# Second layer's cross attention: the scores of two heads issued as a pair, each contracting 32 partitions

## What is computed

```python
def _mha(query, key, value, Wq, bq, Wk, bk, Wv, bv, Wa, ba, mask=None):
    q = (query @ Wq + bq).reshape(Nq, Tq, 16, 16)
    k, v = ...                                   # from the context: 375 rows
    attn = jnp.einsum('bthd,bshd->bhts', q, k) / np.sqrt(16)
    score = jax.nn.softmax(attn, axis=-1)
    y = jnp.einsum('bhts,bshd->bthd', score, v).reshape(Nq, Tq, 256)
    return y @ Wa + ba

t2 = _mha(tgt, tgt, tgt, ..., tgt_mask)          # own attention
x = _layer_norm(tgt + t2, ln1_g, ln1_b)
t2 = _mha(x, memory, memory, ...)                # cross attention
x = _layer_norm(x + t2, ln2_g, ln2_b)
t2 = relu(x @ lin1_W + lin1_b) @ lin2_W + lin2_b
return _layer_norm(x + t2, ln3_g, ln3_b)
```

## Time and profile before

| | us |
|---|---|
| median of 3 runs | 3871.56 |
| the three runs | 3872.68, 3871.56, 3820.96 |
| the profiled execution | 3822.77 |
| its span, first to last instruction | 3821.0 |
| TensorE busy in the span | 3584.9 (94%) |
| VectorE busy | 2020.9 (53%) |
| ScalarE busy | 1746.1 (46%) |
| GpSimd busy | 402.0 (11%) |
| mean granted TensorE clock | 0.963 of full |

### The profile page before, as it was taken

The page is one execution under the profiler, slowest core; times in us unless marked ns, Lnnn a source line. Parts: engine busy times, 40 slices in busy tenths (PEclk is TensorE's granted clock), DMA queues, the critical chain, the costliest instruction groups (busy, mean ns, idle before and its releaser), DMA issues. The chain is left out here.

```text
span 3821.0 us, 67697 instructions
## 1 busy us (share of the span) xinstructions
PE 3584.9 (94%) x21748; PEld 2729.5 (71%) x21748; DVE 2020.9 (53%) x6215; ACT 1746.1 (46%) x4893; POOL 402.0 (11%) x488
## 2 busy tenths in 40 slices
PE   8999999999989999999997999999999997888888
PEld 6778778887867888888775666666676674565565
DVE  4644555464445555556554445445445445657656
ACT  3544545454443333334333545555555453344444
POOL 2101101110101111101101000000000001211111
PEclk9999999999999999999998999999999998898999
DMA  5000000000040000000001000000000000000000
GB/s 199 4 11 14 9 9 12 14 4 12 6 134 12 13 13 13 7 6 13 13 3 49 8 15 8 8 14 8 8 14 8 8 10 14 11 26 13 13 26 5
DMA packets 58462, 75.11 MB, mean 20 GB/s; under 512 B 6752, under 2 KB 55584, under 8 KB 57024
## 3 DMA queue, kind: packets, MB, share of 16 engines
q1 hardware_dynamic: 58176, 71.45, 5.9%
HBM read 64.04 MB, written 7.40 MB: 19 GB/s over the span
## 5 line engine op out<-in xcount | busy, mean ns | idle before, releaser
L161 PE MATMUL l_bank<-l_xT,weights_of_layers_and 128*128 128x224 f32 x2816 | 619.5, 374 | 17.2 <-ACT l_xT L1161 8.0
L161 PEld LDWEIGHTS l_bank<-l_xT,weights_of_layers_and 128*128 128x128 f32 x2816 | 550.1, 201 | 54.0 <-ACT l_xT L1161 8.7
L614 ACT ACTIVATE l_pT<-l_bank 125x336 f32<-125x336 f32 (+2 forms) x736 | 347.1, 472 | 341.0 <-PE l_bank L546 330.3
L546 PEld LDWEIGHTS l_bank<-identity,l_p 112*125 112x125 f32 (+2 forms) x2336 | 334.8, 178 | 184.6 <-issue 96.8
L546 PE MATMUL l_bank<-identity,l_p 112*125 112x112 f32 (+2 forms) x2336 | 390.0, 279 | 21.6 <-DVE l_p L590 18.2
L631 ACT ACTIVATE l_p<-l_p,l_nm 112x375 f32<-112x375 f32 x384 | 233.4, 608 | 284.9 <-DVE l_nm L665 283.8
L161 PE MATMUL l_bank<-l_cT,weights_of_layers_and 128*128 128x375 f32 x832 | 306.3, 495 | 4.7 <-DVE l_z L1811 3.7
L161 PE MATMUL l_bank<-weights_of_layers_and,l_cT 128*125 128x256 f32 (+2 forms) x960 | 301.0, 451 | 0.2
L728 POOL TENSOR_TENSOR l_ve<-l_mv,eps 112x2 f32<-112x2 f32 (+1 forms) x89 | 17.3, 195 | 2548.7 <-DVE l_mv L722 2548.7
L590 DVE TENSOR_SCALAR l_p<-l_p,l_rs 112x375 f32<-112x375 f32 (+1 forms) x608 | 255.1, 420 | 21.7
L568 PEld LDWEIGHTS l_bank<-l_pT,l_cv 125*64 125x64 f32 (+1 forms) x3648 | 163.6, 131 | 138.7 <-issue 98.7
(11 more groups left out here) (253 smaller groups left out, 6118.6 us busy)
## 6 DMA issues: line engine op xcount, KB each, us to landing
l_cT<-in_ctx_turned SPq DMA_DIRECT2D x32, 375.0 KB, 3.4
l_cx<-in_ctx SPq DMA_DIRECT2D x16, 375.0 KB
context_rows<-in_ctx_reversed SPq DMA_DIRECT2D x16, 375.0 KB
tokens<-x_after_layer SPq DMA_DIRECT2D x25, 224.0 KB, 2.6
x_after_layer<-l_z SPq DMA_DIRECT2D x24, 224.0 KB, 2.4
weights_of_layers_and<-bias_lines_kept SPq DMA_DIRECT2D x1, 2625.0 KB, 16.3
weights_of_layers_and<-in_L_xattn_w_fused SPq DMA_DIRECT2D x1, 2048.0 KB, 10.7
weights_of_layers_and<-in_L_xattn_w_ff SPq DMA_DIRECT2D x1, 2048.0 KB, 12.7
```

The source lines that it names most:

```text
L161: last = pe.matmul(out, left, right, start=(k == 0), stop=(k == len(pairs) - 1))
L546: last = pe.transpose(TR.bank(m)[:ph.keys, g * ph.rows:(g + 1) * ph.rows], p[:ph.rows, m % self.p_slots, g * ph.keys:(g + 1) * ph.keys], i ...
L614: return act.activation(out, src, ACT.Copy)
```

## The change

For a phase that isn't grouped (L1's cross phase alone), `scores` does nothing in odd steps. In an even step k it waits for all that items k and k + 1 need, the banks of both among it, and then issues both scores one behind the other, into two banks, each with its own increment. `at` swaps the second and third head of each four, so the order of heads is 0, 2, 1, 3, 4, 6, 5, 7 and so on. `quarter` cuts both operands to the 32 partitions that hold the head and its neighbour, so that the two scores of a pair lie in different groups of 32 partitions (heads 0 and 1 in partitions 0 to 31, heads 2 and 3 in 32 to 63). Transposes, values and what the other engines do keep their order. In `Columns` the same was written with `abreast`, which is 1 everywhere, so that the other layers issue what they did.

```diff
     def at(self, k):
-        return self.batches[k // self.per_batch], k % self.per_batch
+        r = k % self.per_batch
+        if not self.grouped:
+            r += (0, 1, -1, 0)[r % G]
+        return self.batches[k // self.per_batch], r
...
         def scores(ph, k):
+            if not ph.grouped:
+                if k % 2 == 0:
+                    for n in (k, k + 1):
+                        for sem, count in S.free(i, ph.first + n, *ph.ready(n)):
+                            pe.wait_ge(sem, count)
+                    for n in (k, k + 1):
+                        pe.matmul(S.bank(ph.first + n)[:T, 0:S2], ph.q(*ph.at(n)), ph.k(*ph.at(n)), start=True, stop=True).then_inc(S.full.sem, 1)
+                return
             m = ph.first + k
...
-            if ph.grouped:
-                for g in range(G):
-                    last = pe.matmul(bank[:T, g * T:(g + 1) * T], ph.q(j, r * G + g), ph.k(j, r * G + g), start=True, stop=True)
-            else:
-                last = pe.matmul(bank[:T, 0:S2], ph.q(j, r), ph.k(j, r), start=True, stop=True)
+            for g in range(G):
+                last = pe.matmul(bank[:T, g * T:(g + 1) * T], ph.q(j, r * G + g), ph.k(j, r * G + g), start=True, stop=True)
...
+        def quarter(h, a):
+            n = h * DH % 128 // 32 * 32
+            return a[n:n + 32, :]
+
+        cross = Phase("c", False, H, DH, lambda j, h: quarter(h, qz[:, h // HEADS_PER_TILE, h % HEADS_PER_TILE, j * T:(j + 1) * T]),
+                      lambda j, h: quarter(h, ckT[:, j, h // HEADS_PER_TILE, :]), lambda j, h, t: cv[:, j, t, h, :], cross_ready, val_ready=cross_values_ready)
```

More of the change, by code:

```diff
@@ L430, in __init__ @@
     def __init__(self, name, items, dh, rows, q, k, val, ready, val_ready, place, out, bias=None, grouped=False, sides=2, tiles=CT,
-                 turned_by="act", emptied_by="dve", scaled_by="dve", ring=None):
+                 turned_by="act", emptied_by="dve", scaled_by="dve", ring=None, abreast=1):
+        self.abreast = abreast
         self.name, self.items, self.dh, self.rows, self.q, self.k, self.val, self.ready = name, items, dh, rows, q, k, val, ready
@@ L532, in scores @@
         def scores(ph, k):
[L533 to L539, removed]
+            if k % ph.abreast:
+                return
+            width, own = ph.keys * ph.tiles, range(k, k + ph.abreast)
+            for n in own:
+                for sem, count in S.free(i, ph.first + n, *ph.ready(n)):
+                    pe.wait_ge(sem, count)
+            for n in own:
+                for g in range(ph.n):
+                    last = pe.matmul(S.bank(ph.first + n)[:ph.rows, g * width:(g + 1) * width], ph.q(n, g), ph.k(n, g), start=True, stop=True)
+                last.then_inc(S.full.sem, 1)
         def turns(ph, k):
@@ L1469, in layer1 @@
                     bias=lambda r: wide(masked[:, :], 1, G), val_ready=own_values_ready)
-        cross = Phase("c", False, H, DH, lambda j, h: qz[:, h // HEADS_PER_TILE, h % HEADS_PER_TILE, j * T:(j + 1) * T],
-                      lambda j, h: ckT[:, j, h // HEADS_PER_TILE, :], lambda j, h, t: cv[:, j, t, h, :], cross_ready, val_ready=cross_values_ready)
+        def quarter(h, a):
[3 more added lines that the diff above has]
+                      lambda j, h: quarter(h, ckT[:, j, h // HEADS_PER_TILE, :]), lambda j, h, t: cv[:, j, t, h, :], cross_ready, val_ready=cross_values_ready)
         OWN = cross.items
```

## The result

| | before | after |
|---|---|---|
| median, us | 3846.73 (4 runs, 3820.96 to 3872.68) | 4121.59 (4 runs, 4116.16 to 4134.33) |
| span of the profiled execution | 3821.0 | 4123.7 |
| mean granted clock | 0.963 | 0.874 |

The change makes the kernel slower: ratio 1.0741, 95% interval 1.0672 to 1.0809 (the quotient of the two medians, 1.0715, lies inside it).

A forecast was written before the change was run, and what follows sets the result against it. TensorE, busy 94% of the span, was taken to set the pace. With the clock lost, cross adds 293 us and own 86, total 379 on the profiled 3822.77, giving 4202 us; range 4030 to 4300.

The forecast's parts named there:

- Overlap: L1 cross scores: a pair's two scores overlap fully, taking 0.63 us, a saving of 0.63 per pair.
- Switch and settled pair: L1 cross: switching between 32-partition groups and whole array costs 0.30 a pair; settled pair 2.75 us instead of 3.08.
- the held clock: Rival: clock stays 1.00 in cross despite the starting hole; 3797 us, or 3759 with free switches; chance 0.16.
- The wait: Start of each cross phase: pair (2, 3) waits for exponential 0, leaving TensorE a hole of 2.4 us.
- The clock falls about 4 us in: Each cross phase: granted clock drops to 0.50 about 4 us after its start.
- Because of the hole: Start of cross: about 1.2 us busy in the first 3.4, less than in either stall that cost the clock.
- It won't come back by itself: Cross, mostly loads, and own: clock remains at 0.50 until the projections after own.
- Its rival: Clock falls in some turns only, as two matmuls at once may count for more; three of eight 3953 us; chance 0.08.
- Everything doubles: TensorE at clock 0.50: a load costs 0.20 us instead of 0.10, a pair takes 5.5.
- +36.6 a turn for cross: Cross phase takes 85.1 us at the fallen clock, 36.6 more than before; 293 us in 8 turns.
- +12.3 a turn: Own phase: TensorE's busy 14.77 us doubles to 29.5, 12.3 more; 86 us in 7 turns.
- The slower runs of before: Suspected without a row: slower runs of the kernel before lose the clock in one turn, costing 49 us.

The follow-up runs named there:

- quarters with a full start: Changed kernel with items 0 to 2 single over 128 partitions, two extra whole matmuls before item 2, pairs over 32 partitions from item 3: 4087.72 us.
- halves: Changed kernel with paired scores over 64 partitions from item 3, heads reordered, items 0 to 2 whole and single, two extra matmuls before item 2: 3815.39 us.
- the hole alone: Kernel before with one added wait per cross phase: score 1 waits for exponential 0; no pairs, all 128 partitions: 3895.86 us.
- whole pairs: Changed kernel with its pairs, head order and waits, but each score contracting all 128 partitions, so nothing overlaps: 3831.38 us.
- the filled start: Changed kernel with three extra matmuls over 128 partitions ahead of the wait of pair (2, 3) in each cross phase: 4096.78 us.
- the odd pairs: Changed kernel with item 0 alone, pairs (1, 2) to (29, 30), item 31 alone, heads in natural order: 4120.39 us.
- both kernels of single scores: Kernel before with scores over 32 partitions one at a time: 4293.73 us; the same with five extra whole matmuls before score 2: 4305.05 us.
- a thin start: Changed kernel with scores over 64 partitions, heads 0, 4, 1, 5, 2, 6, 3, 7, item 0 alone, then pairs (1, 2) and on: 4122.72 us.
- without the added matmuls: Changed kernel with items 0 to 2 single over 128 partitions, then pairs over 64, heads reordered, no extra matmuls: 3817.84 us.
- three kernels of halves with the two added matmuls: The kernel listed as halves (3815.39 us), and it with item 31 (3792.58 us) or items 29 to 31 (3788.78 us) single over 128 partitions.

## Why the prediction held, and where it didn't

The number was right: 4202 us with 4030 to 4300 was forecast, 4122 came. The direction was right, and so were most of the steps; but the cause that it names is not the one that decides. That the number came out is thus in part luck.

**Overlap.** Full overlap was taken, from four records in column groups. It is so for row groups: four records in 0.89, and the quarters with a full start took the same 2.76 a pair as halves before their clock fell. The rule of the Trainium skill that the prediction weighed, "TensorE: Matmul & The Clock Gate", Part 3, would, as the prediction applied it, have made a pair three passes long, 0.94 from its start to the next transposes at the least. Halves and quarters need 0.82 at full clock, switch included, and the trace of after has the four records over in 0.89, tail included. In which order the passes are issued no trace here shows.

**Switch and settled pair.** 0.63 + 0.30 and two items' rest gave 2.75; halves take 2.76 at full clock. After never ran a settled pair at full clock, so this could be read only in an experiment. (The price of the held clock with free switches, 3822.8 - 26 - 128 x 0.30, is 3758 and not 3759; nothing rests on it.) The Trainium skill's drain on a changed mode, "TensorEngine Tiling (Array Packing)", Key Properties, agrees: the scores of a pair need 1404.71 - 1403.89 = 0.82 until the next transposes start, 0.19 more than their two passes.

**The wait.** The pair (2, 3) waits for exponential 0; a hole of 2.4 us was forecast, 2.17 came.

**The clock falls about 4 us in.** It did (4.2 to 4.3 us in six turns, 2.1 in the first, 3.7 in the last). **Because of the hole:** this step failed as the prediction put it. It compared the new start with the two stalls of the earlier trace rows and found it emptier than both. That is borne out as far as it goes, since the kernel before with the hole alone lost the clock in seven of its eight turns. But filled up, the changed kernel loses the clock as well, and with the hole alone it is back after 3.4 us in six turns of those seven.

**"It won't come back by itself."** The conclusion was true and its reason too wide. The prediction took it from short matmuls in own and put it on the many loads of cross. Cross over 128 partitions won the clock back seven times of eight (six of seven with the hole alone, and the one time that whole pairs lost it); over 32 it never did, in 48 turns of six kernels (after, the filled start, the odd pairs, both kernels of single scores, and the quarters with a full start), nor over 64, in nine turns of two (all eight with a thin start, one without the added matmuls). That fewer partitions lose a clock that was held, and don't win it back, is shown. Why is not: it fits that a score over 32 partitions leaves most of the array unused while TensorE counts as busy, but whole scores, too, stayed at 0.50 in one turn. The prediction weighed the partitions nowhere in its account of the clock. Its rival had the opposite sign ("two matmuls at once may count for more than one").

So the number came out for a reason that stood only half in it. Had the start been filled, as someone who believed the prediction would have done, it would have forecast the held clock, 3797 or so; 4097 was measured.

**Terms mis-sized.** "Everything doubles" at 0.50, 5.5 a pair, was too much: 5.14, which is 1.86 times 2.76. Part by part: scores 1.52 against 0.82, transposes 0.77 against 0.41, six values up to the next start 1.00 against 0.53. A load thus costs 1.00 / 6 = 0.17. The prediction's 0.20 was 1.62 / 8, the whole length of eight merged load records, put against 0.10 from start to start. From start to start the eight take 1.38 in before (the next load starts at 1355.99), which is 0.17 as well. Fourteen pairs x 0.36 = 5.0 of the 6.7 us by which its +36.6 a turn for cross exceeds the 29.9 measured. Outside cross, +12.3 a turn was forecast and +8.8 came. The forecast let the fallen clock last until the projections. It rose earlier, at 1428.60, inside own, behind the product of the cross output: eight records of 256 columns over all 128 partitions. The sixth own score begins 1428.58 - 1407.07 = 21.5 us after the first in after, and 12.5 after it before (1446.26 to 1458.72); that 9.0 is the loss. Both together, 8 x 6.7 + 7 x 3.5 = 78, is the distance from 4202 to 4124.

**The slower runs of before.** The prediction suspected that each run near 3870 us has lost the clock in one turn, at 49 us. Runs now support it. Beside the last five kernels 12 of 41 runs of before lie at 3866 to 3878 us (median 3869.3) with a mean clock of 0.949 to 0.951, the other 29 at 3817 to 3830 (median 3820.8) with 0.960 to 0.965: 48.5 us apart. The lost turn in the kernel with the hole alone, its seventh, took 158.94 us to the next turn's first score, against 114.15 on average for the six turns before it. In before the seventh turn is 3.9 shorter than the six before it (107.91 against 111.78), so the lost turn costs about 158.94 - 110.3 = 48.7. The mean clock fits too, by an estimate: before's profile, at 0.963 over 3821 us, lacks 141 us of full clock, the lost turn's 109.2 us at 0.50 lack 55 more, and 196 of 3869 leaves 0.949. A lost turn was thus profiled in other kernels; no slower run of before was, so for before it stays likely and unshown. The three kernels of halves with the two added matmuls have no run set apart like these in 29.

## What to carry to other kernels

Contracting fewer partitions is no free cut, even when a matmul costs no more for it and two then overlap: TensorE may lose its clock, which here took far more than the overlap gave. Pack narrow matmuls so that they fill the array together (two halves, not two quarters), make the items at both ends of the phase whole where the trace shows the clock lost there, and read the granted clock stage by stage before any busy share. When a mechanism rests on an idle gap, fill the gap first: that one kernel would have shown that something else is at work.

## What the hardware showed that was not expected

- Busy time doesn't tell what the clock follows. Quarters and halves with the same instructions, columns and unbroken busy time: 0.50 against 1.00, 4087.72 against 3815.39 us.
- A fallen clock can hold itself down. Halves keep 1.00 when they begin at 1.00 (1.00 through cross in all eight turns with the full start, 3815.39 us) and stay at 0.50 when a thin start has lost it (all eight turns of the halves with a thin start, 4122.72 us). The same settled pairs run in both. Whole scores, which won the clock back seven times, stayed at 0.50 for 109.2 us once.
- The clock can be lost in one turn of eight with identical work (the seventh turn of the hole alone, 109.2 us at 0.50). What tipped it there is open. All eight turns start alike (0.9 us of work, then 2.25 of waiting); the clock fell 4.56 us after the first score in this one, and 2.6 to 4.4 us after it in the six that recovered.
- Left open: whether the last item of a phase matters by its partitions or by what follows it. Item 31 was widened and the own phase behind it was never changed.
